# Attention values as f32 products in four column tiles, scores in row tiles

## The reference, cut to what matters

```
x = _ln(src) * (1.0 + scale) + shift
q = (x @ Wq + bq)...   # the same for k and v: 16 heads x 512 x 32
scores = einsum('bhqd,bhkd->bhqk', q / sqrt(32), k) + attention_bias
scores = where(src_mask, -inf, scores)
probs = softmax(scores, axis=-1)
ctx = einsum('bhqk,bhkd->bhqd', probs, v)
x = x + (ctx @ Wo + bo)
```

## Time and profile before

| | |
|---|---|
| median of three runs | 3021.0 us |
| profiled execution, its own time | 3018.96 us |
| its span, first to last instruction | 3017.2 us |
| mean granted TensorE clock | 0.974 |
| TensorE matmul busy, whole span | 2772.7 us (92%) |
| VectorE, ScalarE, GpSimd busy | 1905.1, 1121.9, 1030.5 us |

### The profile page before, as it was taken

One profiled execution on the slowest core, in us unless ns is written; L12 is line 12 of the kernel. 1 busy time (PEld: TensorE's weight loads), 2 busy tenths in 40 slices (PEclk: granted clock), 3 DMA queues, 4 the chain that ended last, 5 costly groups with the idle time before them and its releaser, 6 DMA issues. The chain is left out here.

```text
span 3017.2 us, 45792 instructions
## 1 busy us (share of the span) xinstructions
PE 2772.7 (92%) x14016; PEld 2235.5 (74%) x14016; DVE 1905.1 (63%) x3724; ACT 1121.9 (37%) x2256; POOL 1030.5 (34%) x743
## 2 busy tenths in 40 slices
PE   6966999999999999969999999999699999999997
PEld 2425788888888888857787887888577777777775
DVE  8956878777887877756444444443566665665653
ACT  1215778776776768741111111111111111112111
POOL 1004667666766666543101101110332222222210
PEclk9988999999999999999999999999899999999998
DMA  4235676766666676643100000000343333333310
GB/s 165 105 101 177 195 208 181 209 179 201 198 198 192 186 209 179 187 131 98 42 29 12 18 29 29 29 1 14 123 155 95 116 113 107 96 122 105 95 63 35
DMA packets 249524, 356.52 MB, mean 118 GB/s; under 512 B 26554, under 2 KB 105466, under 8 KB 246586
## 3 DMA queue, kind: packets, MB, share of 16 engines
q1 hardware_dynamic: 247546, 350.26, 38.3%
q0 software_dynamic: 1728, 3.16, 0.4%
HBM read 268.94 MB, written 34.05 MB: 100 GB/s over the span
## 5 line engine op out<-in xcount | busy, mean ns | idle before, releaser
L822 POOL TENSOR_TENSOR at_bias<-at_bias,at_mask 128x1024 f32<-128x1024 f32 x224 | 481.1, 2150 | 365.7 <-DMA at_bias<-in_fside_Bx16xSxS 364.1
L1215 DVE TENSOR_TENSOR at_pL<-at_bank_probT,at_pH 128x512 fp32r<-128x512 f32 x512 | 351.2, 686 | 201.5 <-ACT at_pH L931 199.6
L924 ACT ACTIVATE at_y<-at_bias,at_nmax 128x512 f32<-128x512 f32 x512 | 368.5, 720 | 58.9 <-DVE at_nmax L1209 57.3
L931 ACT ACTIVATE at_pH<-at_bank_probT 128x512 fp32r<-128x512 f32 x512 | 304.6, 595 | 197.7 <-PE at_bank_probT L1072 192.1
L1209 DVE CUSTOM_DVE_ANT_0 at_bias<-at_bias,at_bank_score 128x512 f32<-128x512 f32 x512 | 346.1, 676 | 1.0 <-ACT at_y L924 0.9
L1072 PE MATMUL at_bank_probT<-at_ident,at_y 128*128 128x128 f32 x2048 | 310.8, 274 | 34.1 <-DVE at_pL L1215 28.0
L1601 POOL TENSOR_SCALAR expert_WH<-expert_stage 128x1024 fp32r<-128x1024 f32 x128 | 164.3, 1283 | 514.5 <-PE expert_bank_out L98 331.3
L1935 DVE CAST ff_gH<-ff_g 128x512 fp32r<-128x512 f32 x128 | 69.0, 539 | 394.4 <-ACT ff_g L1674 394.4
L1674 ACT ACTIVATE expert_g<-expert_bank_hid,expert_b1c 128x512 f32<-128x512 f32 x128 | 88.3, 690 | 617.6 <-PE expert_bank_hid L98 617.6
L1674 ACT ACTIVATE ff_g<-ff_bank_hid,ff_b1c 128x512 f32<-128x512 f32 x128 | 88.3, 689 | 616.6 <-PE ff_bank_hid L98 616.6
L1072 PEld LDWEIGHTS at_bank_probT<-at_ident,at_y 128*128 128x128 f32 x2048 | 245.7, 141 | 95.6 <-ACT at_y L924 27.3
(11 more groups left out here) (320 smaller groups left out, 6284.7 us busy)
## 6 DMA issues: line engine op xcount, KB each, us to landing
at_bias<-in_fside_Bx16xSxS SPq DMA_DIRECT2D x256, 512.0 KB, 4.6
expert_stage<-in_L_cond_Wi SPq DMA_DIRECT2D x128, 256.0 KB, 2.7
expert_stage<-in_L_cond_Wo SPq DMA_DIRECT2D x128, 256.0 KB, 2.8
at_q<-at_nat SPq DMA_DIRECT2D x384, 64.0 KB, 3.6
at_k<-at_nat SPq DMA_DIRECT2D x384, 64.0 KB, 3.1
st_f<-in_x SPq DMA_DIRECT2D x8, 1024.0 KB, 7.0
x_after_layer<-st_y SPq DMA_DIRECT2D x8, 1024.0 KB, 4.8
at_x<-x_after_layer SPq DMA_DIRECT2D x32, 256.0 KB, 4.2
```

The source lines that it names most:

```text
L822: pool.tensor_tensor(bias[i % NB][:, :, :], bias[i % NB][:, :, :], mask[:, 2 * i % R:2 * i % R + 2, :], ALU.add).then_inc(s_bm, 1)
L924: act.activation(prob[u % 2][:, :], bias[u // 2 % NB][:, u % 2, :], ACT.Exp, scale=-1.0, bias=nmax[:, u % 4:u % 4 + 1], accum_out=sums[:, ...
L931: act.activation(pH[u // 2 % 2][:, :, u % 2, :], pT[u % 2][:, :].rearrange("p (k q) -> p k q", q=P), ACT.Copy).then_inc(s_pth, 1)
L1215: dve.tensor_tensor(pL[u // 2 % 2][:, :, u % 2, :], pT[u % 2][:, :].rearrange("p (k q) -> p k q", q=P), f32(pH[u // 2 % 2][:, :, u % 2, :] ...
```

## The change

The order of units within a chunk becomes query tile outside, head inside, so that four neighbouring units are the four heads of one chunk for one query tile (a *group*).

- Values: v stays plain f32, without a high and a low part. A group takes 16 products: for each of four key blocks, four heads, each with 32 stationary columns in its own column tile and 128 moving columns of probabilities; the four heads write 32 partitions each of one context bank. Eight are issued in the second unit after the group, eight in the third (values, called with (0, 1) and (2, 3)).
- Probabilities: the transposed ones are only copied, even units by ScalarE (copy_even), odd ones by VectorE (copy_odd). probs_high and probs_low go, and so do v_low, copy_low and add_high; one copy of the whole context bank for a chunk comes in (copy_ctx).
- Scores: the stacks and their DMAs go. Two heads' scores are made at once by six products with 32 rows each, alternately in two row tiles and two banks, from the unstacked high and low parts of q and k. They are issued before the transposes of an even unit, for the two units after the next.
- Output projection: one chunk at a time, three products for each of four query tiles at units 12, 14 and 15 of the next chunk, and each result is added to x at once (add_part), so 16 additions a batch element in place of four.
- Buffers: one context bank instead of two, three pJ banks instead of two, xH and xL double, bias loads bring two heads of one query tile instead of two query tiles of one head.

```diff
-        v = [sb(f"v{s}", [P, 2 * R, 7, HD], F32R) for s in range(2)]
+        xH = [sb(f"xH{s}", [P, C, S], F32R) for s in range(2)]
+        v = [sb(f"v{s}", [P, R, P]) for s in range(2)]
...
-            def scores(n, u):
...
-                pe.matmul(pS[u % 2][:, :], q3[:, j, r * P:(r + 1) * P], k3[:, j, :],
-                          start=not masked, stop=True).then_inc(s_qk, 1)
...
+            def scores(n, p):
+                c, r, j = p // (UC // 2), p // 2 % R, p % 2 * 2
+                if p % (UC // 2) == 0:
+                    pe.wait_ge(s_ql, n * C + c + 1)
+                    pe.wait_ge(s_kl, n * C + c + 1)
+                wait_count(pe, s_max, n * NU + 2 * p)
+                masked = p % NP in ON_PE
+                if p % NP == min(ON_PE):
+                    pe.wait_ge(s_mask, (n + p // NP) * 2 + 2)
                 if masked:
-                    pe.matmul(pS[u % 2][:, :], ident16[:, :], mask[:, r, :], start=True, stop=False)
-                pe.matmul(pS[u % 2][:, :], q3[:, j, r * P:(r + 1) * P], k3[:, j, :],
-                          start=not masked, stop=True).then_inc(s_qk, 1)
+                    for bank in pS:
+                        pe.matmul(bank[:, :], ident16[:, :], mask[:, r, :], start=True, stop=False)
+                parts = ((qH[c % 2], kH[c % 2]), (qL[c % 2], kH[c % 2]), (qH[c % 2], kL[c % 2]))
+                for k, (q, key) in enumerate(parts):
+                    for s in range(2):
+                        rows = slice((j + s) * HD, (j + s + 1) * HD)
+                        mm = pe.matmul(pS[s][:, :], q[rows, r * P:(r + 1) * P], key[rows, :], start=k == 0 and not masked, stop=k == 2)
+                mm.then_inc(s_qk, 1)
...
-            def values(n, p):
-
-                h, half = divmod(p, 2)
-                t, g = divmod(h, 2)
-                c = h // HC
-                pe.wait_ge(s_ptl, n * NU + 2 * p + 2)
-                if p % 8 == 0:
-                    pe.wait_ge(s_vl, n * C + c + 1)
-                if p % 4 == 0 and not (is_first(n) and t < 2):
-                    pe.wait_ge(s_add, n * NT + t - 1)
-                for k in range(4):
-                    for part, probs in enumerate((pH, pL)):
-                        mm = pe.matmul(pC[t % 2][:, half * 2 * P:(half + 1) * 2 * P],
-                                       v[c % 2][:, k * 2 + t % 2, 3 * g:3 * g + 4, :].rearrange("p b d -> p (b d)"), probs[p % 2][:, k],
-                                       start=(p % 4 == 0 and k == 0 and part == 0), stop=(p % 4 == 3 and k == 3 and part == 1))
-                mm.then_inc(s_pv, 1)
+            def values(n, g, ks):
+
+                c, r = divmod(g, R)
+                if ks[0] == 0:
+                    for s in range(2):
+                        pe.wait_ge(s_pt[s], n * NP + 2 * g + 2)
+                if r == 0 and ks[0] == 0:
+                    pe.wait_ge(s_vc, n * C + c + 1)
+                    wait_count(pe, s_cc, n * C + c)
+                for k in ks:
+                    for j in range(HC):
+                        d = slice(j * HD, (j + 1) * HD)
+                        mm = pe.matmul(pC[d, r * P:(r + 1) * P], v[c % 2][:, k, d], probT[g % 2][:, j, k, :], start=k == 0, stop=k == R - 1)
+                if ks[-1] == R - 1:
+                    mm.then_inc(s_pv, 1)
...
+            fill_at = {0: (0,), 2: (1,), 3: (2, 3)}
+            y_at = {12: (0,), 14: (1,), 15: (2, 3)}
+            x_at = {41: 0, 42: 1, 46: 2, 49: 3}
...
+                    if cur and u % 2 == 0 and (u + 2 < NU or nxt):
+                        scores(n, u // 2 + 1)
...
+                    if u % HC == 1 and (prev or u > 1) and (cur or u == 1):
+                        values(n, (u - 5) // HC, (0, 1))
+                    if u % HC == 2 and (prev or u > 2) and (cur or u == 2):
+                        values(n, (u - 6) // HC, (2, 3))
...
-            def probs_low(n, u):
-                dve.wait_ge(s_pth, n * NU + u + 1)
-                if u % 2 == 0 and not (is_first(n) and u < 4):
-                    dve.wait_ge(s_pv, n * NP + u // 2 - 1)
-                dve.tensor_tensor(pL[u // 2 % 2][:, :, u % 2, :], pT[u % 2][:, :].rearrange("p (k q) -> p k q", q=P),
-                                  f32(pH[u // 2 % 2][:, :, u % 2, :]), ALU.subtract).then_inc(s_ptl, 1)
...
+            def copy_odd(n, u):
+                g, j = divmod(u, HC)
+                dve.wait_ge(s_tp, n * NU + u + 1)
+                if j == 1:
+                    wait_count(dve, s_pv, n * NG + g - 1)
+                dve.tensor_copy(probT[g % 2][:, j].rearrange("p k q -> p (k q)"), pT[1][:, :]).then_inc(s_pt[1], 1)
...
+            def copy_ctx(n, c):
+
+                act.wait_ge(s_pv, n * NG + (c + 1) * R)
+                wait_count(act, s_cl, n * C + c)
+                act.activation(pv, pC[:, :], ACT.Copy).then_inc(s_cc, 1)
...
-            def stack(n, c, j, t, halves):
-
-                if not (is_first(n) and c == 0):
-                    sp.wait_ge(s_qk, n * NU + ((c - 1) * HC + j + 1) * R)
-                for g, half in enumerate(halves):
-                    sp.dma_start(f32(t[g * HD:(g + 1) * HD, j, :]), f32(nat[half][j * HD:(j + 1) * HD, :])).then_inc(s_rep[j], 16)
...
+                c, r, j = i // (UC // 2), i // 2 % R, i % 2 * 2
+                h = c * HC + j
+                sp.dma_start(bias[i % NB][:, :, :], a["fside_Bx16xSxS_0"][ds(m, 1), h:h + 2, r * P:(r + 1) * P, :].rearrange("a h p k -> (a p) h k")).then_inc(s_bias[i % NB], 16)
```

More of the change, by code:

```diff
@@ L573, in attention @@
         pT = [ps(f"probT{s}") for s in range(2)]
-        pC = [ps(f"ctx{s}") for s in range(2)]
-        pJ = [ps(f"proj{s}") for s in range(2)]
+        pC = ps("ctx")
+        pJ = [ps(f"proj{s}") for s in range(3)]
         s_id = sem("ident_steps")
@@ L733, in _ @@
                     load_bias(0, 2)
-            for j in range(HC):
-                stack_q(0, 0, j)
-                stack_k(0, 0, j)
             def body(n, slot, prev, nxt, units):
@@ L775, in _ @@
             pool.memset(mhalf[:, :], -0.5).then_inc(s_cm, 1)
-            for s in range(2):
-                pool.memset(f32(v[s][:, :, 1:6:2, :]), 0.0).then_inc(s_cm, 1)
             for k, name in enumerate(("bq", "bk", "bv")):
@@ L848, in body @@
                         add_mask(m, i)
[L849 removed]
+                    if nxt and u == 29:
                         power(n + 1)
@@ L1116, in steps @@
                     if ks[0] == 0:
-                        banks[kind] = bank(n, (kind, c), prev, nxt, cur)
+                        banks[kind] = bank(n, kind, c, prev, nxt, cur)
                     for k in ks:
-                        project(n, kind, c, k, banks[kind])
-                def y_steps(r, ks):
-                    if ks[0] == 0:
-                        banks["y"] = bank(n, ("y", r), prev, nxt, cur)
-                    for k in ks:
-                        project_y(n - 1, r, k, banks["y"])
+                        project(n, slot if c < C else 1 - slot, kind, c, k, banks[kind])
@@ L1127, in body @@
                 for u in range(units):
                     c, it = divmod(u, UC)
+                    make = cur and (nxt or c < C - 1)
+                    spread = (prev or c > 0) and (cur or c == 0)
+                    if cur and u % 2 == 0 and (u + 2 < NU or nxt):
+                        scores(n, u // 2 + 1)
                     if cur:
                         transpose_probs(n, u)
[L1131 to L1134 removed]
@@ new lines, in body @@
+                    if make and 4 <= it < 8 and it - 4 in fill_at:
+                        steps("k", c + 1, fill_at[it - 4])
+                    if make and 8 <= it < 12 and it - 8 in fill_at:
+                        steps("w", c + 1, fill_at[it - 8])
+                    if spread and it == 5:
+                        spread_inverses(n, c - 1, bank(n, "i", c - 1, prev, nxt, cur))
+                    if spread and it in y_at:
+                        for r in y_at[it]:
+                            project_y(n, c - 1, r, bank(n, "y", (c - 1, r), prev, nxt, cur))
```

384 lines of the change are left out of this document (149 added, 235 removed), and 7 rows, old and new, of the table uses.

## The result

The changed kernel takes 3042.88 us (median of six runs, 3037.73 to 3047.78) against 3020.38 us for the kernel before in the same six rounds: a ratio of 1.0072, 95% interval 1.0059 to 1.0086. It is 22.5 us slower. The forecast was 2980 us, faster by 1.3%: the sign was wrong, and all of the loss is in attention.

A forecast was written before the change was run, and what follows sets the result against it. TensorE's list was taken to bound attention. Four units: 4.58 unchanged + 1.45 scores + 1.3 values + 0.3 shape changes + 0.47 hole = 8.10 against 8.35 us, -32 us over 128 groups, -8 at the end: 2980 us, range 2860 to 3090.

The forecast's parts named there:

- What bounds the kernel: Steady attention: TensorE's list sets the time, busy 962.96 of 1000 us; work taken from other engines gives next to nothing.
- Values: Sixteen plain f32 value products in column tiles: 1.3 us for four units, from 0.86 to 1.48, against 1.92 before.
- The floor by weight loads: Value products: loading weights for 32 short f32 records might keep four units from going below 1.48 us.
- two tiles deep: Rival on value products: in-order starts let only two records run at a time, 1.71 us, total 3031; chance 0.24.
- no overlap: Rival on value products: column tiles run one after another, 3.42 us for four units, total 3250; chance 0.12.
- Scores: Six products per two heads, row tiles side by side: 1.45 us for four units, from 1.40 to 2.80, against 1.28.
- Changes between tile shapes: TensorE switching between full-width and tiled products: eight changes in four units, 0.3 us, bounds 0 and 0.72.
- The row that spoke for nothing: Earlier trace, 32 stationary columns to full width: an ordinary distance of 0.23 us, taken to show a change costs nothing.
- Waits: TensorE in four units: 0.25 us of low-part and stack waits go, 0.15 comes for VectorE's sums between score pairs.
- The end of the stage: Output projection after the last context: 12 products remain instead of 48, about 3 us instead of 12, so -8 us.
- the hole: TensorE time in four units beyond the summed products, idle time and uncovered weight loads: 0.57 us before, 0.47 forecast.
- something else that costs: Rival: some other cost, such as score-pair waits several times the 0.15 us allowed; chance 0.05.

The follow-up runs named there:

- x's low parts early: The changed kernel, with VectorE making the low parts of x's chunks 1 and 2 one unit earlier (units 43 and 47): 3014.0 us, 0.999 of the kernel before.

## Why the prediction was wrong, step by step

- *What bounds the kernel*: right. TensorE's list set the time; 173 us less of VectorE in 1000 gave nothing.
- *Values*: four column tiles at once, 0.86 us of streaming for a group. That is the lower bound; 1.3 was taken, 0.44 too much. The floor by weight loads does not exist here: the loads of other tiles go beside the streaming. The rivals of two tiles deep and of no overlap are both refuted by the 0.57 us of a half.
- *Scores*: side by side as forecast, 1.40 of streaming in four units; 1.45 was taken.
- *Changes between tile shapes*: this is the step that failed. 0.3 us in four units was taken, 0.72 was the bound, and 1.25 is what the edges add up to in the trace: 0.32 and 0.31 for the two halves of the values, 0.26 for the scores behind values, 0.36 for the scores behind a projection. Of this 1.10 goes in a group without waits when the same streaming is done at full width, and 131 us, 1.02 for each group, in all. The count of changes was one too high (seven, not eight), which is not where it failed: seven at 0.09 are 0.63. The row that spoke for nothing was misread: products named 128\*32 in the earlier trace rows have 32 stationary columns and are followed by full-width work at 0.23, without an edge, unlike the column-tiled products of the same name, after which it comes 0.14 late. That row says nothing of leaving four column tiles. And I priced one event for a change, the 0.09 of the earlier trace rows, where a burst has three: the entry, about 0.10; its own first load, 0.11 in the scores (the load records show the first set of weights starting with its products at 706.15 and the second 0.11 later); and the exit, 0.09 to 0.14 with 0.06 in the transposes behind. The Trainium skill ("TensorEngine Tiling (Array Packing)", Key Properties) states that a change of mode drains the engine. The prediction held the rows against it. This trace agrees in that every change costs time, 0.10 us for an entry from a projection; that it is a drain that costs it no row shows.
- *Waits*: 0.15 us in four units were allowed for the score pairs' wait, and in the regular chunks 0.03 came: 0.13 once in 16 units, where the scores start 0.70 us behind the values' first start instead of 0.57. The waits that came were not in the sum: units 44, 48 and 49, 4.4 us in a batch element or 0.27 in four units, 29 us in all. I had looked at what stands between two sums, and not at what the new bank table puts behind a bank that VectorE reads late. The granted clock of the window, 0.98, is 1.00 with x's low parts early, so part of the 29 us is clock that came back behind the idle times: 24 us less at half clock are worth at most 12 us.
- *The end of the stage*: right, 8.6 us gained against 8.
- *Untouched stages*: zero was forecast, 10.5 us less measured; at most 7 by the clock, the rest open.

By the sum: 8.10 predicted, less 0.44 and 0.05 for streaming, plus 1.25 - 0.30 = 0.95 for edges and 0.27 for waits, is 8.83 against 8.75 measured; the rest is the hole, set at 0.47. The forecast's own test had named it: six score products were to start within 0.7 to 0.8 us and took 0.89, and the first instruction after values, to be "no more than 0.1 late", is 0.14 late.

That 3043 lies inside the stated range, and inside the span given for two tiles deep (3005 to 3060), is luck: the mechanism of that rival is refuted, and what happened was priced only as "something else that costs", with a chance of 0.05.

## What to carry to other kernels

Count the bursts, not the products: a run of tiled matmuls pays about 0.3 us at its edges here, whether it has eight records or thirty-two, so tiled work should be long, and tiled work of one kind should stand next to that of the other. Before splitting work into parts to smooth a list, price the edge of each part; before joining them, look at which engine's result the next burst needs. When a table of shared banks is rewritten, walk it once for each bank to see which engine reads it last and behind what; two misplaced reads cost more here than the whole change lost.

## What was not expected of the hardware

Plain f32 products in four column tiles run fully at once: eight products, sixteen records, in 0.57 us with the edge at their end included, and thirty-two in 706.94 - 705.93 = 1.01. Although each product is two records, the records of four heads interleave: they start in fours, within 0.02 us, and the fours are 0.11 to 0.13 us apart. The shape printed beside a product does not tell whether an edge follows: in the earlier trace rows the step from 32 stationary columns back to full width has none, and here it has one. The two also differ in type and length, and no run separates what makes the difference.
